# A new order of steps in the steady loop of a four-layer convolution-block kernel, with layer 1's scores in a PSUM bank of their own

## The reference

```
x = x + L0(gn(x))   # quantize: nearest of 1024 codes (matmul 256x1024, argmin), then take that code's row
x = x + L1(gn(x))   # f, g = x Wf, x Wg (32 wide); h = x Wh; attn = sigmoid(f g^T) along each 64-pixel row; attn h
x = x + L2(gn(x))   # x0, x1, x2 = x w1, x w2, x w3 per pixel; softmax over n of x0[n]*x1[m], n, m = 4096;
                    # feats[m] = sum_n x2[n] softmax; sigmoid(feats) * x
x = x + L3(gn(x))   # linear attention, 4 heads of 32: softmax(q) over d, softmax(k) over pixels,
                    # context = k v^T, out = context q, projection, layer norm
```

## Time and profile before

| | |
|---|---|
| median of 3 runs | 5604.9 us (5603.44 to 5609.42) |
| the profiled execution's own time | 5609.25 us |
| its span | 5607.3 us |
| granted TensorE clock, mean over the span | 0.966 |
| busy: PE, DVE, ACT, POOL | 94%, 73%, 71%, 34% |
| DMA | 38 GB/s, 211.22 MB |

### The profile page before, as it was taken

How to read it: one execution, slowest core, us unless ns; L and a number is a source line. 1 busy time by engine, 2 the same in 40 slices (tenths; PEclk the granted TensorE clock), 3 DMA queues, 4 the chain that set the end, 5 groups by cost and what they waited for, 6 DMA issues and landing times.

```text
span 5607.3 us, 113930 instructions
## 1 busy us (share of the span) xinstructions
PE 5256.8 (94%) x44520; PEld 2738.1 (49%) x44520; DVE 4116.6 (73%) x8686; ACT 3974.4 (71%) x6017; POOL 1925.3 (34%) x1588
## 2 busy tenths in 40 slices
PE   7799999999999999999999999999999999999996
PEld 3436445364553645446364553645446364453624
DVE  8467677777777777677777777777777776777726
ACT  1467868677785877868677785877858678676795
POOL 3224243342423424243341423424234251433403
PEclk9899999999999999999999999999999999999997
DMA  2010201102011020201102011020201102011000
GB/s 85 6 40 11 67 26 50 38 6 72 20 61 31 17 64 14 66 26 39 47 7 71 22 61 31 13 67 14 64 28 32 52 11 67 26 45 41 7 31 31
DMA packets 163252, 211.22 MB, mean 38 GB/s; under 512 B 13216, under 2 KB 146080, under 8 KB 162720
## 3 DMA queue, kind: packets, MB, share of 16 engines
q1 hardware_dynamic: 138144, 136.79, 7.6%
q0 software_dynamic: 24576, 67.14, 4.1%
HBM read 136.78 MB, written 67.11 MB: 36 GB/s over the span
## 4 chain that ended last, share of the span: by engine, by line
PE 67%; ACT 13%; DVE 11%; issue 6%; POOL 2%; DMA 1%; ACTq 0%; DVEq 0%; POOLq 0%; SPq 0%
PE PS L1185 33%; PE PS L1362 15%; PE PS L1353 6%; ACT n_x L510 3%; DVE stats L839 2%; PE PS L1461 2%; PE PS L1219 2%; PE PS L1243 2%; PE PS L1296 2%; ACT xin L510 2%; ACT big L582 2%; ACT work L549 1%; ACT attn L559 1%; ACT soft L582 1%; DMA quant_H<-emb_t,idx 1%
## 5 line engine op out<-in xcount | busy, mean ns | idle before, releaser
L582 ACT ACTIVATE big<-PS 128x1024 f32<-128x1024 f32 x1376 | 1365.8, 1024 | 463.5 <-PE PS L1353 401.8
L582 ACT ACTIVATE soft<-PS 128x1024 f32<-128x1024 f32 x672 | 676.1, 1024 | 352.9 <-PE PS L1353 345.2
L405 POOL DMA_INDIRECT quant_H<-emb_t,idx x512 | 487.5, 952 | 979.9 <-DVE idx L863 788.2
L1185 PE MATMUL PS<-e_hi,n_hi 128*128 128x512 f16 x2048 | 781.4, 382 | 17.5 <-POOL n_lo L398 8.5
L1185 PE MATMUL PS<-e_lo,n_hi 128*128 128x512 f16 x2048 | 778.0, 380 | 0.0
L1185 PE MATMUL PS<-e_hi,n_lo 128*128 128x512 f16 x2048 | 777.8, 380 | 0.0
L1362 PE MATMUL PS<-big,w 128*4 128x512 f32 x5504 | 756.8, 639 | 0.0
L839 DVE BATCH_NORM_STATS2 stats<-XT 128x6 f32<-128x512 f32 x1024 | 651.8, 683 | 14.5 <-POOL XT L421 4.9
L863 DVE FIND_INDEX8 idx<-m,work 128x8 uint32<-128x1024 f32 x512 | 622.1, 1219 | 0.0
L1353 PE MATMUL PS<-rhs,lhs 12*128 12x512 bf16 x4096 | 558.3, 395 | 60.9 <-ACT big L582 38.6
L857 DVE CUSTOM_DVE_ANT_0 work<-PS,e_bias,m 128x512 f32<-128x512 f32 x512 | 384.0, 750 | 211.7 <-PE PS L1185 205.8
(11 more groups left out here) (208 smaller groups left out, 10795.1 us busy)
## 6 DMA issues: line engine op xcount, KB each, us to landing
xin<-x SPq DMA_DIRECT2D x128, 512.0 KB, 3.9
out<-yout SPq DMA_DIRECT2D x128, 512.0 KB, 2.9
quant_H<-emb_t,idx POOLq DMA_INDIRECT x512, 2.7
XT<-emb SPq DMA_DIRECT2D x1, 1024.0 KB, 6.1
XT<-wh SPq DMA_DIRECT2D x1, 256.0 KB, 5.7
XT<-wqv SPq DMA_DIRECT2D x1, 256.0 KB, 5.8
XT<-wk SPq DMA_DIRECT2D x1, 128.0 KB, 5.7
w_sb<-w SPq DMA_DIRECT2D x1, 128.0 KB, 5.3
```

Source lines behind the costliest of these rows:

```text
L405: nc.gpsimd.indirect_dma_start(quant[:, g % 2, u, :], None, emb_t, bass.IndirectOffsetOnAxis(ap=idx[:, t % (2 * GT), 0:1], axis=0),).then_ ...
L582: nc.scalar.activation(E[h % 3][:, z * 1024:(z + 1) * 1024], bank(2 * z, 2), ACT.Exp).then_inc(exped.sem, 1)
L1185: ins = mm(dst, a, b, start=first and j == 0, stop=last and j == 2)
```

## The change

Three kinds of edit. (1) Layer 1's scores go to bank 2; `l1_fg` waits for the copy of the group before instead of its tanh; `l1_scores` gets two waits and `l3_qv` one, which keep bank 2 from being overwritten. (2) The loop bodies of POOL, ACT, DVE and PE are laid out in a new order. The same steps stand in them; `prepare`, empty after image 0, is also named. (3) Prologue, last block and SP's lists are unchanged.

```diff
-        l1_fged, l1_fgkept, ... = step("l1_fged"), step("l1_fgkept"), ...
+        l1_fged, l1_fgkept, ... = step("l1_fged"), step("l1_fgkept", NG, 1), ...
 # ACT, l1_tanh
-                nc.scalar.activation(tanhs[:, g % 2, :], PS[:, 4, 0:GT * ROW], ACT.Tanh, scale=0.5)...
+                nc.scalar.activation(tanhs[:, g % 2, :], PS[:, 2, 0:GT * ROW], ACT.Tanh, scale=0.5)...
 # PE, l1_fg
-                pe.wait_ge(*l1_tanhed.room(im, g, 1))
+                pe.wait_ge(*l1_fgkept.room(im, g, 1))
 # PE, l1_scores
+                if g == 0 and im > 0:
+                    pe.wait_ge(*gate_arg.after(im - 1))
+                pe.wait_ge(*l1_tanhed.room(im, g, 1))
                 pe.wait_ge(*l1_fgkept.after(im, g))
-                        ins = mm(PS[r * ROW:(r + 1) * ROW, 4, cols], ...
+                        ins = mm(PS[r * ROW:(r + 1) * ROW, 2, cols], ...
 # PE, l3_qv
+                if g == 0 and im + 1 < B:
+                    pe.wait_ge(*l1_tanhed.after(im + 1, NG - 1))
```

The order around the start of the scores, on ACT and on PE, and the places where other steps change place:

```diff
 # ACT
-                exp(old, 31, 1); l0_norm(new, 0, 0); l0_norm(new, 0, 1); exp(old, 32, 0); l0_norm(new, 0, 2)
-                l0_norm(new, 0, 3); exp(old, 32, 1); exp(old, 33, 0); exp(old, 33, 1); l0_norm(new, 1, 0)
+                exp(old, 31, 1); l0_norm(new, 0, 0); l0_norm(new, 0, 1); l0_norm(new, 0, 2); l0_norm(new, 0, 3)
+                exp(old, 32, 0); exp(old, 32, 1); l0_norm(new, 1, 0); l0_norm(new, 1, 1); l0_norm(new, 1, 2)
+                l0_norm(new, 1, 3); exp(old, 33, 0); exp(old, 33, 1); l0_norm(new, 2, 0); exp(old, 34, 0)
...
-                l1_norm(new, 1); gate_chain(old, 1); gated(old, 1); l1_fg(new, 0); l1_norm(new, 2); gated(old, 2)
-                l1_tanh(new, 0); l1_fg(new, 1); l1_norm(new, 3); l1_tanh(new, 1); gated(old, 3); gated(old, 4)
+                l1_norm(new, 1); gate_chain(old, 1); l1_fg(new, 0); gated(old, 1); gated(old, 2); l1_tanh(new, 0)
+                l1_norm(new, 2); l1_fg(new, 1); l1_norm(new, 3); gated(old, 3); l1_tanh(new, 1); l1_fg(new, 2)
...
+                l1_norm(new, 7); l1_fg(new, 5); l1_fg(new, 6); l1_tanh(new, 5); l1_tanh(new, 6); l1_fg(new, 7)
 # PE
-                fill(old, 2, 1); fill(old, 3, 0); l3_qturn(last, 6); sums(old, 1)
-                fill(old, 3, 1); combine(last, 1); fill(old, 4, 0); combine(last, 2); fill(old, 4, 1)
+                fill(old, 2, 1); fill(old, 3, 0); sums(old, 1)
+                fill(old, 3, 1); combine(last, 1); l3_qturn(last, 6); fill(old, 4, 0); combine(last, 2)
...
                 sums(old, 30)
-                sums(old, 31)
-                fill(old, 32, 1); fill(old, 33, 0); sums(old, 32)
-                fill(old, 33, 1); fill(old, 34, 0); score(new, 0, 0); score(new, 0, 1); fill(old, 34, 1)
+                fill(old, 32, 1); sums(old, 31)
+                fill(old, 33, 0); fill(old, 33, 1); sums(old, 32)
+                score(new, 0, 0); score(new, 0, 1); score(new, 1, 0); fill(old, 34, 0); fill(old, 34, 1)
...
-                l1_h(new, 6, 0); l1_fg(new, 6); l1_h(new, 6, 1); l1_scores(new, 6); gn(old, 3, 1); l1_fg(new, 7)
+                l1_h(new, 6, 1); l1_fg(new, 6); gn(old, 3, 1); l1_fg(new, 7); l1_scores(new, 6); gn(old, 3, 2)
...
-                l3_ctx(old, 3); piece_turn(new, 0); l3_kturn(old, 4); l3_qturn(old, 2); piece_turn(new, 1)
+                l3_kturn(old, 3); l3_k(old, 4); l3_qturn(old, 1); l3_ctx(old, 2); l3_qv(old, 4); l3_kturn(old, 4)
+                piece_turn(new, 0); l3_qturn(old, 2); piece_turn(new, 1); l3_ctx(old, 3); l3_k(old, 5)
 # POOL
-                l0_norm(new, 1, 3); index(new, 0); index(new, 1); index(new, 2); index(new, 3); index(new, 4)
-                l0_norm(new, 2, 3); index(new, 5); l0_norm(new, 3, 3); index(new, 6); index(new, 7); index(new, 8)
-                index(new, 9); index(new, 10); index(new, 11); l0_norm(new, 4, 3); index(new, 12); index(new, 13)
+                index(new, 0); l0_norm(new, 1, 3); index(new, 1); l0_norm(new, 2, 3); index(new, 2); index(new, 3)
+                index(new, 4); index(new, 5); index(new, 6); index(new, 7); index(new, 8); index(new, 9)
+                l0_norm(new, 3, 3); l0_norm(new, 4, 3); index(new, 10); index(new, 11); index(new, 12)
```

More of the change, by code:

```diff
@@ L1104, in _ @@
[L1104 to L1105 removed]
+                combine(last, 2); final_sq(last, 0); l3_qsoft_(last, 7); final_sq(last, 1); final_out(last, 0)
+                final_out(last, 1); final_sq(last, 2); l3_qturn(last, 7); turn_in(new, 0); final_sq(last, 3)
+                final_sq(last, 4); turn_in(new, 1); final_out(last, 2); final_out(last, 3); final_sq(last, 5)
@@ L1517, in _ @@
-                final_z(last, 6); final_out(last, 4); turn_in(new, 3); fill(old, 14, 1); fill(old, 15, 0)
-                sums(old, 13)
+                final_z(last, 3); turn_in(new, 0); fill(old, 10, 0); fill(old, 10, 1); sums(old, 8)
+                final_out(last, 2); final_z(last, 4); fill(old, 11, 0); fill(old, 11, 1); sums(old, 9)
+                turn_in(new, 1); fill(old, 12, 0); sums(old, 10)
+                final_z(last, 5); fill(old, 12, 1); fill(old, 13, 0); sums(old, 11)
+                final_out(last, 3); sums(old, 12)
@@ L1530, in _ @@
-                sums(old, 20)
+                fill(old, 18, 0); fill(old, 18, 1); final_z(last, 9); final_out(last, 7); fill(old, 19, 0)
+                turn_in(new, 6); sums(old, 17)
+                final_z(last, 10); final_out(last, 8); fill(old, 19, 1); fill(old, 20, 0); sums(old, 18)
+                turn_in(new, 7); final_z(last, 11); fill(old, 20, 1); sums(old, 19)
+                fill(old, 21, 0); final_out(last, 9); turn_in(new, 8); final_z(last, 12); fill(old, 21, 1)
+                fill(old, 22, 0); sums(old, 20)
@@ L1562, in _ @@
+                fill(old, 40, 1); fill(old, 41, 0); score(new, 10, 1); turn0(new, 3); score(new, 11, 0)
+                score(new, 11, 1); score(new, 12, 0); turn0(new, 4); score(new, 12, 1); fill(old, 41, 1)
+                fill(old, 42, 0); sums(old, 39)
                 sums(old, 40)
@@ L1614, in _ @@
-                l3_ctx(old, 4); l3_k(old, 6); l3_qv(old, 6); l3_k(old, 7); l3_kturn(old, 6); piece_turn(new, 3)
-                l3_qturn(old, 4); piece_turn(new, 4); l3_qv(old, 7); l3_ctx(old, 5); l3_qturn(old, 5)
-                l3_ctx(old, 6)
+                spread(old, 1); spread(old, 2); l1_scores(new, 0); l1_h(new, 1, 0); l1_h(new, 1, 1); l1_fg(new, 1)
+                l1_out(new, 0); l1_scores(new, 1); spread(old, 3); l1_h(new, 2, 0); l1_h(new, 2, 1); l1_fg(new, 2)
+                l1_out(new, 1); l1_scores(new, 2); l1_h(new, 3, 0); l1_fg(new, 3); l1_h(new, 3, 1); spread(old, 4)
@@ L1617, in _ @@
+                l3_qv(old, 5); piece_turn(new, 2); piece_turn(new, 3); l3_qturn(old, 3); l3_kturn(old, 5)
+                l3_ctx(old, 4); l3_k(old, 6); l3_qv(old, 6); l3_kturn(old, 6); l3_ctx(old, 5); l3_k(old, 7)
+                l3_qturn(old, 4); piece_turn(new, 4); l3_qv(old, 7); l3_qturn(old, 5); l3_ctx(old, 6)
             old, last = B - 1, B - 2
```

259 lines of the change are left out of this document (120 added, 139 removed).

## The result

The changed kernel takes 5711.8 us (median; 5691.7 to 5721.3), the kernel before, run beside it, 5607.2 (5603.4 to 5611.0): ratio 1.0182, 95% interval 1.0153 to 1.0210. I had forecast 5586 and a range that ended at 5624. The profiled execution took 5713.06 us, its span is 5711.1.

What follows compares the result with a forecast made beforehand. PE, busy 94% of the span, was taken as the bound, with losses in three short low-clock stretches. Terms summed to -1.25 us per image, times 15 = -19 us, giving 5586 us on the median; eight-in-ten range 5545 to 5624.

Steps and rivals of the forecast that it cites:

- Layer 1's bank: Layer 1's scores in bank 2: l1_fg no longer waits for the previous group's tanh; -0.2 us per image.
- Layer 1's order: Layer 1: ACT does gated(2) and tanh(0) ahead of norm(2); with the bank -0.3 us per image, bounds -1.0 to +1.0.
- Group-norm chain: Before the scores: n_hi ahead of exp(32,0), fill(32,1) before sums(31), first score 1.36 us earlier; -1.0 per image, bounds -1.4 and 0.
- Scores and gathers: Score stage: POOL does norm passes ahead of or after index steps; 0 us per image, bounds -0.3 and +2.1.
- Pieces: l3_kturn(4) placed before piece_turn(0), which waits for POOL; -0.45 us per image, bounds -0.45 and 0.
- Seam: Between images: l3_qturn(6) behind combine(1) delays combine(2), ACT's qturn copy and exp(4,0); +0.5 us per image, bounds 0 and +1.0.
- Pairs and swaps: Loop's paired fills, 76 slots becoming 77, other neighbours' swaps, turn_in and final_out; 0 us per image, bounds -0.5 and +0.5.
- The price of one half: PE's time at 1.2 instead of 2.4 GHz: about half is lost, 6.7 of 13.4 us per image.
- the third: Late beat of 341.3 us becomes all images' through more half rate: 3.4 us on 11 more images, 5623 us; 17%.
- the fourth rival: New waits: terms set at 0 cost what bounds allow, POOL pass +2.1, seam +1.0; +1.0 per image, 5620 us; 11%.
- The first rival: The clock's falls pin the beat, so saved time is given back: 5600 to 5609, say 5604 us; 20%.
- layer 1's gain: A further bank for layer 1 could give clock back; zero, since layer 1 runs at 1.00 over its 62.10 us.

Runs made afterwards that it cites:

- the run with less work: Kernel before without four score matmuls per image (n_hi by e_lo, tiles 20 and 24, images 1 to 15): 5601.0 us, ratio 0.9990.
- both kernels with new scores: Kernel before with bank edit and the changed kernel's whole score stage: 5607.1 us; the same with PE's last 20 steps of that stage old: 5600.8 us.
- the busy-work runs: 15 extra unread transposes per image on PE (8 in the seam, 7 around group norm): changed kernel 5722.7 us, kernel before 5604.0 us.
- the start alone: Kernel before with the bank edit and the new order only at the start of the scores, their rest old: 5656.3 us, ratio 1.0089.
- old finals: Changed kernel with only the finals' stage put back in its old order on every engine: 5670.7 us, ratio 1.0102.
- old layer 3: Changed kernel with only layer 3's stage put back in its old order on every engine: 5669.6 us, ratio 1.0126.
- the pair on ACT swapped back: Changed kernel with one pair on ACT in old order again, l1_tanh(1) ahead of gated(3): 5719.9 us, ratio 1.0202.
- more work: Kernel before with four score matmuls per image done twice (n_hi by e_hi, same tiles as with less work): 5630.1 us, ratio 1.0043.

## Why the prediction was wrong

Point by point, by its own steps.

- **Layer 1's bank, -0.2.** 0. The wait on the tanh went, and layer 1 stayed at 55.96.
- **Layer 1's order, -0.3 with the bank, bound +1.0.** +1.3 without a fall, +2.8 with the fall that starts as l1_h(4,0)'s wait of 1.9 us ends (clock 0.50 from 2590.3 us on). The wait alone doesn't make the fall: the third image has it too, at a clock of 1.00. I followed the first group only. DVE is busy 48 of 56 us there; gated(5) came late on ACT, gating(5) on DVE after it, and l1_h(4,0) needs the bank that DVE's l1_out(2) empties; in the same way ACT's copies of f and g came late for l1_scores(5) and (7), 1 us per image. I had named DVE as a cap on the gain and not as the way a loss travels, and had looked at ACT's copies nowhere. By which swap the 1.3 us come isn't shown: ACT's list or one pair of it put back left them.
- **Group-norm chain, -1.0.** Right in mechanism, and near in size: the first score comes 1.1 earlier instead of 1.36, and the stage takes 1.0 less with the scores changed alone. Right too that the fall there stays (0.93 in both). As a gain of the whole it was worth nothing.
- **Scores and gathers, 0.** Right in the undisturbed image (108.45 against 108.47), though fill(63,0) waits 0.6 longer, which I hadn't seen. The 0.9 us per image of gather waits was a mean of 0.4 and of a few late gathers of 2 to 3 us.
- **Pieces, -0.45.** 0.04 came. The stage around it, for which I had no other term, cost +1.3: l3_qturn(5) waits for DVE 0.7 us per image. I had priced one wait of a list in which a dozen steps changed place.
- **Seam, +0.5.** About 0: +0.1 undisturbed, and old or new order makes no difference. combine(2) comes 0.8 later only where half rate stretches it.
- **Pairs and swaps, 0, bounds -0.5 to +0.5.** The first large miss: +2.5. I counted slots over the whole loop (76 to 77), and the two that the finals lost were paid, while the two fewer in the rest of the scores went against that wait ahead of fill(63,0). And I set the swaps of final_out, final_z and turn_in between PE and DVE at 0 without matching the two lists step by step.
- **The sum.** The step that failed most is the one under all terms: that the falls of the clock stay as they are and that microseconds add. In the undisturbed image the terms should have come to +3.6; in a steady one, with 31 us at 1.2 GHz instead of 14, the loss is 10.3. The price of one half for each such microsecond was wrong as well: 0 in the seam of the kernel before, some 0.4 between the changed kernel's two images.

Of the rivals the third, more time at half rate, took place, at 17%. I placed it at the end of the scores; it came in the seam, the finals, the end of the scores and layer 1, and my price of 3.4 us per image was the difference between two beats of the old order, half of the 6.6 found. Those slow beats come with late gathers in three of four images, and the changed kernel has one such image (1.9 us). It came on top of new waits, the fourth rival, and I had priced each only alone, the third with the forecast's gain of 19 us still in it. The fourth's sum was wrong too: half a POOL pass (1.05) with the seam's 0.5, which was in the sum already, gives -0.2 per image and not +1.0. The first rival, that the beat holds, is right for small savings: the run with less work and both kernels with new scores show it.

The Trainium skill ("TensorE: Matmul & The Clock Gate", section "A second HAM failure mode: psum-queue depth-cycling"), which I had weighed only for layer 1's gain, says that a PE which idles briefly between groups of matmuls, there because a loop cycles through PSUM banks, sees its clock go back and forth. That agrees in kind with the busy-work runs (0.63 to 0.89 in the seam), though the idle pieces here are waits for ACT and DVE, and with layer 1, where l1_h(4,0) waits 1.9 us and the fall follows in most images; read against the change, it spoke of the loss.

What stays open: why the steady beats of so many orders come near four values (337.9 with the bank alone and the new scores; 341.3 with the start alone; 344.7 with old finals and with old layer 3; 348.2 in the changed kernel and with the pair on ACT swapped back), when other runs mix them or keep to none (340.7 with more work; 345.2, 347.0 and 348.6 with busy work). Why a gather is late in single images isn't shown either. The runs show that a change in one stage is answered by the length of a fall in another; they don't show by what rule, nor how much of the 6.6 us the falls cost by themselves. Which of the new waits lengthens the seam's fall wasn't separated beyond the stage.

## What to carry to other kernels

When the clock already falls in places, a sum of microseconds is a forecast only for an order that leaves every wait ahead of those places alone; otherwise read the time at 1.2 GHz and the waits as two accounts, and look for an image in the same trace where only one differs. Before a single long stretch is put down to an experiment, look at the same stretch of the same image in the kernel before. For a new order, match the lists of both engines step by step in every stage: three unremarked swaps cost more than the one chain that I followed gained. Here a saving in a stage nearly free of waits returned nothing to the beat, and a cost there more than itself.

## What the runs showed of the hardware

- 0.9 us of matmuls removed per image left the beat at 337.9 us in the mean; 0.9 us added made it 340.7.
- Two images of one execution with the same instructions differ by 6.6 to 7 us, with 31 and 14 us at 1.2 GHz. But such time can be free: the seam of the kernel before takes 12.67 us at a clock of 0.87 and, with transposes that nobody reads in its gaps, at 1.00; and with the new scores alone an image takes 338.0 us with some 10 or some 17 us of it.
- PE's waits for gathers come to some 0.4 us in most images of the kernel before and to 3.0 us in the one from 4192 us on (2.6 the longest), which takes 342.1 us instead of 337.9.
